# Scaling one head of two in an attention kernel, and turning a unit's first tile one slot earlier

## The reference

```python
x = x + tanh(g_xattn[0]) * attention(layernorm(x), ctx, ...)
x = x + tanh(g_ffn[0]) * ffn(layernorm(x), ...)
# attention, for every head h:
#   scores = q_r @ k_r^T              (64 wide)
#   attn   = softmax(scores)          (over 1024 keys)
#   ctx_c  = attn @ kv_rope           (128 wide)
# out = sum over h of (ctx_c @ w_kc_kv[h]^T) @ Wo[:, h]^T
```

## Time and profile before

| | |
|---|---|
| Median of 3 runs | 660.46 us (658.91 to 662.21) |
| The profiled execution | 660.33 us, span 658.5 us |
| TensorE busy | 637.6 us (97%) |
| VectorE busy | 538.6 us (82%) |
| GpSimd busy | 427.3 us (65%) |
| ScalarE busy | 420.3 us (64%) |
| Scaling on GpSimd (L1195) | 128 operations, 146.7 us |

### The profile page before, as it was taken

The page is one execution under the profiler, slowest core; times in us unless marked ns, Lnnn a source line. Parts: engine busy times, 40 slices in busy tenths (PEclk is TensorE's granted clock), DMA queues, the critical chain, the costliest instruction groups (busy, mean ns, idle before and its releaser), DMA issues.

```text
span 658.5 us, 10048 instructions
## 1 busy us (share of the span) xinstructions
PE 637.6 (97%) x2968; PEld 393.1 (60%) x2968; DVE 538.6 (82%) x870; ACT 420.3 (64%) x693; POOL 427.3 (65%) x368
## 2 busy tenths in 40 slices
PE   8799999999999999999999999999999999999997
PEld 7564556666766666666666646575655444445553
DVE  5777887788878887889798978898889986998863
ACT  2564686377747765766666756666665732598875
POOL 4834588767756775676578965776677254686651
PEclk9999999999999999999999999999999998999999
DMA  8208975888598949884988697878689671000001
GB/s 288 79 5 196 288 193 139 230 210 228 147 243 237 240 118 247 253 224 123 232 238 218 189 237 212 217 197 233 172 220 252 171 173 68 0 1 32 17 35 48
DMA packets 45208, 112.79 MB, mean 171 GB/s; under 512 B 11888, under 2 KB 15088, under 8 KB 45040
## 3 DMA queue, kind: packets, MB, share of 16 engines
q1 hardware_dynamic: 42128, 104.24, 59.8%
q10 hardware_dynamic: 2976, 8.06, 3.9%
q0 software_dynamic: 64, 0.00, 0.0%
HBM read 45.16 MB, written 2.10 MB: 72 GB/s over the span
## 4 chain that ended last, share of the span: by engine, by line
PE 56%; DVE 24%; issue 5%; ACT 5%; SPq 4%; DMA 3%; POOL 3%; PEld 1%; ACTq 0%; POOLq 0%; DVEq 0%; PEldq 0%
PE ps_s L1447 9%; DVE small L1853 7%; DVE E L1863 6%; PE ps_s L619 5%; PE ps_b L1480 5%; SPq L1129 4%; PE ps_ctx L1480 4%; PE ps_b L1343 3%; PE ps_b L1398 3%; PE ps_b L1345 3%; PE ps_b L1344 3%; ACT E L1676 2%; PE ps_b L1417 2%; PE ps_b L670 2%; DVE x_sb L1847 2%
## 5 line engine op out<-in xcount | busy, mean ns | idle before, releaser
L1195 POOL TENSOR_SCALAR E<-E,small 128x1024 f32<-128x1024 f32 x128 | 146.7, 1148 | 156.1 <-DVE small L1858 154.2
L1676 ACT ACTIVATE E<-ps_s,small 128x1024 f32<-128x1024 f32 x128 | 142.4, 1115 | 150.5 <-DVE small L1853 134.4
L1237 POOL TENSOR_TENSOR G_lo<-G,g_hi 128x512 fp32r<-128x512 f32 x130 | 168.2, 1308 | 6.7 <-ACT g_hi L1622 6.4
L1863 DVE STREAM_TRANSPOSE E<-E 128x1024 f32<-128x1024 f32 x124 | 152.4, 1231 | 21.8 <-POOL E L1195 21.5
L1853 DVE TENSOR_REDUCE small<-ps_s 128x1 f32<-128x1024 f32 x128 | 149.4, 1206 | 24.3 <-PE ps_s L1447 24.3
L1622 ACT ACTIVATE g_hi<-G 128x512 fp32r<-128x512 f32 x130 | 76.9, 632 | 3.9 <-DVE wq L1879 3.9
L1343 PE MATMUL ps_b<-b_hi,ctx_hi 128*128 128x512 f32 x128 | 66.5, 520 | 0.5 <-DVE ctx_lo L1819 0.3
L1480 PE MATMUL ps_b<-G,kv 128*128 128x512 f32 x126 | 64.7, 609 | 2.1 <-DMA G<-E 2.1
L1480 PE MATMUL ps_ctx<-G,kv 128*128 128x512 f32 x126 | 64.6, 607 | 0.3 <-POOL kv L1229 0.3
L1447 PE MATMUL ps_s<-k_hi,q_hi 64*128 64x512 f32 x256 | 57.3, 444 | 4.8 <-ACT E L1676 3.7
L619 PE MATMUL ps_s<-wq,q12T 128*128 128x512 fp8e4 x256 | 60.6, 383 | 0.1
(11 more groups left out here) (204 smaller groups left out, 1212.0 us busy)
## 6 DMA issues: line engine op xcount, KB each, us to landing
G<-E SPq DMA_DIRECT2D x496, 128.0 KB, 2.5
w_stage<-in_wffn SPq DMA_DIRECT2D x37, 512.0 KB, 4.7
w_stage<-in_wffn ACTq DMA_DIRECT2D x11, 512.0 KB, 4.6
wo_s<-in_woT SPq DMA_DIRECT2D x8, 512.0 KB, 5.2
wq_s<-in_wq SPq DMA_DIRECT2D x7, 512.0 KB, 4.9
wkcq_s<-in_wkcqT SPq DMA_DIRECT2D x7, 384.0 KB, 3.2
out<-x_sb SPq DMA_DIRECT2D x8, 256.0 KB, 2.0
x_sb<-in_x SPq DMA_DIRECT2D x3, 512.0 KB, 6.6
```

Of the source, the lines that this page charges most:

```text
L1195: nc.gpsimd.tensor_scalar(e, e, rowinv[:, k:k + 1], 1.0, ALU.mult, ALU.mult).then_inc(scaled, 1)
L1237: nc.gpsimd.tensor_tensor(g_tile(w % 2, i, G_lo), tile, high_part(i).bitcast(F32).rearrange("p (t i q) -> p t i q", t=ST, i=4), ALU.subtra ...
L1676: nc.scalar.activation(out, scores, ACT.Exp, bias=negmax[:, k:k + 1], accum_out=rowsum[:, k:k + 1]).then_inc(exp_done, 1)
L1863: nc.vector.transpose(e_tile(w % 2, t), e_tile(w % 2, t)).then_inc(blocks_turned, 1)
```

## The change

GpSimd scales the odd tiles alone, by the reciprocal of their own sum times the sum of the even tile beside them: the second head is brought to the scale of the first. The even tiles stay unscaled. Their reciprocals go to columns of their own, `row_scale`, one for each unit and half, and the output rows are multiplied by them when they are added to `x_sb` (`scaled_out`). The gate's tanh, which stood there, is multiplied into `b_hi` and `b_lo`. The transpose of an even tile waits for its exponential alone. `scaled` counts 8 for a pair where it counted 16.

In the order of the work two things move. VectorE turns u3's tile 0 at the end of the slot, behind its reciprocal and low(7), and no longer at the head of the next slot. The reciprocal of u2's tile 1 goes from the head of the slot to behind the maxima of tiles 2 and 3.

```diff
@@ -235,6 +238,7 @@
         negmax = small[:, 64:72]
         rowsum = small[:, 72:80]
         rowinv = small[:, 80:88]
+        row_scale = small[:, 25:33]
         ln_mv = small[:, 96:112].rearrange("p (t c) -> p t c", c=2)
         ln_rstd = small[:, 112:120]
         ln_eps = small[:, 120:128]
@@ -949,8 +953,7 @@
             for s in range(2):
                 dve.wait_ge(side_done, LAST_SIDE + s + 1)
                 x = x_sb[:, 6 + s, :]
-                nc.vector.scalar_tensor_tensor(x, ps_b[:, s, :], g_tanh[:, 0:1], x, ALU.mult, ALU.add)\
-                    .then_inc(side_freed if s == 0 else side_read, 1)
+                scaled_out(dve, PAIRS - 1, 3, s, ps_b[:, s, :], x).then_inc(side_freed if s == 0 else side_read, 1)
 
             dve.sem_inc(et_free, ET_FREE0)
@@ -1186,13 +1189,14 @@
             ffn_sp(sp)
 
 
-        def pool_scale(pool, p, w, t):
-
+        def pool_scale(pool, p, w, s):
+
+            t = 2 * s + 1
             e = first_e(t) if is0(p) and w == 0 else e_tile(w % 2, t)
             k = (w % 2) * ST + t
             pool.wait_ge(inv_done, 16 * p + (4 * w + t + 1))
             pool.sem_inc(pool_passed, 1)
-            nc.gpsimd.tensor_scalar(e, e, rowinv[:, k:k + 1], 1.0, ALU.mult, ALU.mult).then_inc(scaled, 1)
+            nc.gpsimd.tensor_scalar(e, e, rowinv[:, k:k + 1], rowsum[:, k - 1:k], ALU.mult, ALU.mult).then_inc(scaled, 1)
 
         def xn_half(i):
             b, h = divmod(i, 2)
@@ -1239,14 +1243,13 @@
 
         def pool_pair(pool, p, last=False):
             for w in range(4):
-                second, first = not (last and w >= 2), not (last and w >= 1)
-                u2, u3 = unit_ahead(p, w, 2), unit_ahead(p, w, 3)
+                second, u2 = not (last and w >= 2), unit_ahead(p, w, 2)
                 if splits(p, w):
                     split_low(pool, p, w, 0)
                 if splits(p, w):
                     split_low(pool, p, w, 1)
                 if second:
-                    pool_scale(pool, *u2, 1)
+                    pool_scale(pool, *u2, 0)
                 if last and w == 0:
                     join_kv(pool, 1)
                 if splits(p, w):
@@ -1256,8 +1259,7 @@
                 if last and w == 3:
                     rms_root(pool, 1)
                 if second:
-                    pool_scale(pool, *u2, 2)
-                    pool_scale(pool, *u2, 3)
+                    pool_scale(pool, *u2, 1)
                 if last and w == 2:
                     rms_root(pool, 0)
                     pool.wait_ge(ld_g, 32)
@@ -1275,8 +1277,6 @@
                     split_kv(pool, KV_SPLIT_SLOTS.index(w))
                 if isinstance(p, int) and (p, w) == (PAIRS - 2, 3):
                     join_kv(pool, 0)
-                if first:
-                    pool_scale(pool, *u3, 0)
                 if last and w == 1:
                     atanh_end(pool)
@@ -1320,13 +1320,9 @@
             root(2)
             normed_row(6)
             normed_row(7)
-            for t in range(ST):
-                pool_scale(pool, 0, 0, t)
-            pool_scale(pool, 0, 1, 0)
-            pool_scale(pool, 0, 1, 1)
-            pool_scale(pool, 0, 1, 2)
-            pool_scale(pool, 0, 1, 3)
-            pool_scale(pool, 0, 2, 0)
+            for w in range(2):
+                for i in range(2):
+                    pool_scale(pool, 0, w, i)
             pool_pair(pool, 0)
             with pool.Fori(1, XN_JOIN_PAIR) as p:
                 pool_pair(pool, p)
@@ -1589,7 +1585,8 @@
             task(6)
             pe.wait_ge(xnt_copied, 6)
             task(7)
-            pe.wait_ge(scaled, ST)
+            pe.wait_ge(exp_done, ST)
+            pe.wait_ge(scaled, 2)
             pe.wait_ge(xnt_copied, 8)
             first_turn(0)
             first_turn(1)
@@ -1638,7 +1635,9 @@
             elif kind == "a":
                 last = copy_act(a_hi[:, :, :].rearrange("p c r -> p (c r)"), bank_in)
             else:
-                last = copy_act(b_hi[:, task[1], :], bank_in)
+                if is0(p):
+                    act.wait_ge(gate_ready, 1)
+                last = nc.scalar.activation(b_hi[:, task[1], :], bank_in, ACT.Copy, scale=g_tanh[:, 0:1])
             last.then_inc(side_hi, 1)
 
         def xn_high_part(act, i):
@@ -1818,6 +1817,11 @@
 
             return nc.vector.tensor_tensor(out, full, hi.bitcast(F32), ALU.subtract)
 
+        def scaled_out(dve, p, u, i, bank_in, x):
+
+            dve.wait_ge(inv_done, 16 * p + (4 * u + 2 * i + 1))
+            return nc.vector.scalar_tensor_tensor(x, bank_in, row_scale[:, 2 * u + i:2 * u + i + 1], x, ALU.mult, ALU.add)
+
         def side_low(dve, p, variant, task, bank_in, at=None, hi_at=None):
 
             kind = task[0]
@@ -1841,10 +1845,11 @@
                 rows = query_rows(task)
                 last = lo_part(q_lo[:, task[1], rows], bank_in[:, 0:rows.stop - rows.start], q_hi[:, task[1], rows])
             elif kind == "b":
-                last = lo_part(b_lo[:, task[1], :], bank_in, b_hi[:, task[1], :])
+                last = nc.vector.scalar_tensor_tensor(b_lo[:, task[1], :], bank_in, g_tanh[:, 0:1], b_hi[:, task[1], :].bitcast(F32),
+                                                      ALU.mult, ALU.subtract)
             else:
                 x = x_sb[:, 2 * task[1] + task[2], :]
-                last = nc.vector.scalar_tensor_tensor(x, bank_in, g_tanh[:, 0:1], x, ALU.mult, ALU.add)
+                last = scaled_out(dve, p - 1 if task[1] == 3 else p, task[1], task[2], bank_in, x)
             last.then_inc(side_freed, 1)
 
         def max_tile(dve, p, w, t):
@@ -1855,11 +1860,15 @@
         def inv_tile(dve, p, w, t):
             dve.wait_ge(exp_done, 16 * p + (4 * w + t + 1))
             k = (w % 2) * ST + t
-            nc.vector.reciprocal(rowinv[:, k:k + 1], rowsum[:, k:k + 1]).then_inc(inv_done, 1)
+            inv = rowinv[:, k:k + 1] if t % 2 else row_scale[:, 2 * w + t // 2:2 * w + t // 2 + 1]
+            nc.vector.reciprocal(inv, rowsum[:, k:k + 1]).then_inc(inv_done, 1)
 
         def turn_blocks(dve, p, w, t):
 
-            dve.wait_ge(scaled, 16 * p + (4 * w + t + 1))
+            if t % 2:
+                dve.wait_ge(scaled, 8 * p + (2 * w + t // 2 + 1))
+            else:
+                dve.wait_ge(exp_done, 16 * p + (4 * w + t + 1))
             nc.vector.transpose(e_tile(w % 2, t), e_tile(w % 2, t)).then_inc(blocks_turned, 1)
 
         def ctx_low(dve, p, w):
@@ -1898,10 +1907,6 @@
                                 round_half(dve, q, g)
 
                 queries = (task_before(variant, w, 1) or ("",))[0] == "q"
-                if second:
-                    inv_tile(dve, *u2, 1)
-                    if not opening:
-                        turn_blocks(dve, *u2, 0)
                 low(0)
                 if variant == "last":
                     ffn_dve_early(dve, w, 0)
@@ -1914,6 +1919,8 @@
                 if second:
                     max_tile(dve, *u2, 2)
                     max_tile(dve, *u2, 3)
+                if second:
+                    inv_tile(dve, *u2, 1)
                 if opening:
                     turn_blocks(dve, *u2, 0)
                     turn_blocks(dve, *u2, 1)
@@ -1957,6 +1964,8 @@
                 if first:
                     inv_tile(dve, *u3, 0)
                 low(7)
+                if first:
+                    turn_blocks(dve, *u3, 0)
                 if variant == "last":
                     ffn_dve_early(dve, w, 7)
```

## The result

The changed kernel took 666.72 us, the median of 5 runs (666.15 to 670.59), against 660.36 for the kernel before: a ratio of 1.0101, with an interval of 1.0075 to 1.0128. That is 6.4 us slower where 0.8 was forecast, and 2.2 above the end of the range. The profiled execution is one of the two long ones, 669.21 us with a span of 667.4; the three runs at a granted clock of 1.000 took 666.15, 666.23 and 666.72.

A forecast was written before the change was run, and what follows sets the result against it. The prediction took the attention part to be bound by TensorE until the last pair of heads, with VectorE close behind. Its terms, -0.9 + 0.5 + 1.2 = +0.8 us, gave 661.2 us, range 657.5 to 664.5.

The forecast's parts named there:

- The forecast wait: VectorE ahead of tile 1's transpose: 1.2 us dead in slots 0 and 2, waits for GpSimd staying near 20 us.
- rival C: GpSimd's scaling with two columns is slow, 1.55 us, so the dead wait is 1.6: 662.8 us, chance 0.12.
- Start of pair 1: Low parts behind GpSimd's scaling start 1.1 us earlier and both TensorE gaps close: -0.9 us, bounds 0 and -1.0.
- The mean's product: Slot 3 of a summing pair: the x_sb row the mean waits for comes later, +0.5 us once, bounds 0 and +0.75.
- The last pair: Slot 1's new dead wait delays the transposes and the last exchange: +1.2 us, bounds +0.8 and +1.7.
- Three us of cover: GpSimd's low part of key tile 2, done by 432.3, wanted by TensorE at 435.28: the 1.4 us delay stays hidden.
- In slots bound by TensorE this costs nothing: VectorE's moved wait costs nothing where TensorE is packed, as long as exponentials are ready for the next scores.
- the 0.5 us of room given to the scores: Next slot 0 in a quantising pair: a 0.3 us shift of the exponentials is hidden, over 0.5 isn't.
- rival D: VectorE's dead wait passes the scores' room; TensorE waits for exponentials in the middle pairs: 664.7 us, chance 0.12.
- slot 0 wins 1.2 back at its head: The head wait of slot 0 goes in every pair, gaining 1.2 us: the argument against rival D.
- The list of gaps: TensorE gaps that a shift on VectorE or GpSimd could close: 0.5, 0.33, 0.69, 1.67 and 2.15, in all 5.3 us.
- Rival B: VectorE sets the pace from 392 us on and its 21.5 us of waits are mostly saved: 655.1 at best, chance 0.09.

The follow-up runs named there:

- scale3_short: The changed kernel with GpSimd's scaling of tile 3 cut to 32 of its 1024 columns: 663.49 us, 661.1 at full clock.
- fill_behind: inv1_head with an idle 1.2 us maximum on VectorE behind the reciprocal of tile 3, ahead of the transpose of tile 2: 668.73 us.
- turn2_short: The changed kernel with VectorE's transpose of tile 2 cut to 32 of its 1024 columns: 663.70 us, 662.1 at full clock.
- turn0_short: The changed kernel with the transpose of the first tile, at the end of the slot, cut to 32 of 1024 columns: 668.07 us, 666.5 at full clock.
- both_short: The changed kernel with the cuts of scale3_short and turn2_short together: 654.84 us; its control, the same cuts in inv1_head, took 652.66 us.
- inv1_head: The changed kernel with the reciprocal of tile 1 put back at the head of VectorE's slot: 654.7 us, ratio 0.9909 to the kernel before.
- arith_only: The changed kernel's arithmetic in VectorE's old order, reciprocal of tile 1 and transpose of tile 0 both back at the head: 654.85 us.
- lows_first: The changed kernel with GpSimd's low parts of key tiles 2 and 3 ahead of the scalings of tiles 1 and 3: 664.91 us.
- after_again: The changed kernel, unaltered, run and profiled once more: 670.08 us, 666.13 in the one run at full clock.

## Why the prediction was wrong

**The forecast wait was right.** 64 scalings of 1.205 us, median (1.2 was taken, bounds 1.1 and 1.55); VectorE stands 1.2 us ahead of tile 1 in slots 0 and 2, 25 us in sum ("near 20"). The prediction's estimate of 1.54 us, worked out from the Trainium skill ("GPSIMD Engine Reference", section "Performance versus the Vector engine"), is not met by the 1.205 measured, and rival C falls.

**The single terms mostly were, some by halves.** Start of pair 1: true gaps 0.50 and 0.33 before, 0.26 and none after, so -0.6 of the -0.9 there. The mean's product:

```profile
305.79 0.40 PE L1472 MATMUL ps_b<-G_lo,kv_hi 128*128 128x512 f32 x1
307.22 0.37 PE L1491 MATMUL ps_b<-small 128*128 128x24 f32 x2 [1.02 <-DVE x_sb L1823]
```

The true gap is 1.19, against 0.69: +0.5, as forecast. The last pair:

```profile
512.25 1.10 PE L1476 MATMUL ps_ctx<-G,kv 128*128 128x512 f32 x2 [0.63 <-POOL kv L1233]
...
529.43 0.50 PE L1443 MATMUL ps_s<-k_hi,q_hi 64*128 64x512 f32 x2 [0.92 <-ACT E L1675]
...
553.04 1.59 PE L1476 MATMUL ps_b<-G,kv 128*128 128x512 f32 x2 [1.91 <-DMA G<-E]
```

The scores that waited 1.67 us at 512.62 start at 520.10 without a wait. Over the whole pair the shift against before grows from 8.3 us (the scores at 505.87 against 497.56) to 8.9 (553.04 against 544.11): +0.6 for a forecast +1.2. The sign that was named for it, a wait of over 3 us ahead of the last exchange's products, didn't come: that wait is 1.91 us (truly 2.07), near the 2.15 before. Two waits that the prediction didn't list are here: kv, whose halves GpSimd joins behind the late scaling (0.63; 0.28 before, at 503.17), and the scores of slot 1.

**The step that failed is "Three us of cover".** It read GpSimd's room once, in slot 3, at the low part of key tile 2, and took it for every slot. The row of work behind that low part, a scaling and two more low parts, was not followed to TensorE. In slot 2 it ended 0.05 us ahead of its use before the change. The prediction itself gave the price for that case: without cover the delay "would fall on TensorE in every slot". So a term was put at nothing that is several us. The gaps ahead of low-part products alone are 3.2 us, and taking 1.1 us out of that row (scale3_short) gives back 5.1 at full clock.

**"In slots bound by TensorE this costs nothing" failed as well**, with the 0.5 us of room given to the scores. fill_behind and turn2_short show that VectorE has a share: the stretch from the maxima to the transpose of tile 3 has no room for 1.2 us. By which path it reaches TensorE in the changed kernel is open. Behind that stretch stand the exchange and the next maxima, hence the exponentials. In fill_behind TensorE waits for exponentials, which is rival D's mechanism (0.12). In the changed kernel D's sign is missing: between 120 and 529 us no scores have idle time of 0.15 us or more ahead of them, and the waits left for VectorE's lateness are those for b_lo, x_sb and the exchanges. The dead wait at the head that went was no counterweight: turn0_short shows that time just ahead of the head is free, so "slot 0 wins 1.2 back at its head" was worth little or nothing.

Together: the late reciprocal costs 11.5 us (666.2 against 654.7 at full clock). One cut gives back 5.1, the other 4.1, both 11.5, of which 2.0 are what they give where nothing is late. That the late reciprocal costs this much, and that time on both engines must be given back to undo it, is shown. An exact split is not: the two delays feed each other, and the stall before 458 goes with either cut. both_short also stays 2.1 us above its control (654.7 against 652.7 at full clock), where at most 1 was expected; that stays open.

**The arithmetic was priced at -0.9 and gains 5.5.** The list of gaps took the stretches to 304 and from 392 and left out the one between, where the kernel before has 2.2 us of idle time. 1.54 of it (truly 1.86) is a stall that inv1_head reduces to 0.57 (truly 0.73). Before:

```profile
388.66 1.12 PE L1480 MATMUL ps_b<-G,kv 128*128 128x512 f32 x2 [0.15 <-DMA G<-E]
391.18 3.27 PE L1417 MATMUL ps_b<-xn_rows,a_full 128*128 128x512 f32 x7 [1.39 <-DVE b_lo L1819]
```

inv1_head:

```profile
388.46 2.84 PE L1413 MATMUL ps_b<-xn_rows,a_full 128*128 128x512 f32 x6 [0.57 <-DVE b_lo L1848]
```

That stall is 1.1 us of the gain. By the last exchange inv1_head is 3.5 us ahead of the kernel before (540.62 against 544.11), and the other 1.7 of the 5.2 between the two profiles is the lower clock that follows in the kernel before. Runs of it at full clock are also 5.5 behind; where those lose is not shown. Rival B, VectorE's waits saved and gaps closing, had 655.1 at best and 0.09 for a chance. The 654.85 of arith_only, where the wait doesn't move, is close to that, but its list of gaps was another one, so the nearness of the numbers is partly luck.

## What to carry to other kernels

Before a wait is moved, follow the whole row of work queued behind it on its engine to the last consumer, in each kind of slot: the room at the first item says nothing of the fourth. An engine at 54% can have no room in the one stretch between a late input and a fixed due time, and VectorE's time, free at the head of the slot, cost up to 0.5 us for each 1.2 put in between the maxima and the last transpose (14 us over 29 slots in fill_behind, the lower clock's part included). To test which of two coupled delays costs, take time out at each place alone and at both, with a control that takes it out where nothing is late; reordering mostly renamed the wait. And look at each cut's profile for where its gain arises: here over half of it was one stall for an exchange.

## What the hardware showed beyond that

A pause of TensorE can cost more than itself. In the kernel before, the last exchange's wait (544.11, true gap 2.15) is followed by a lower granted clock. The rows are the profile cut into stretches of 5 us; the clock is the third number from the end.

```profile
540.00:545.00 5.00, 2.91 (x13) 1.23 (x12) 4.89 (x13) 1.51 (x2) 0.70 (x1) 0.91 0.93 244
545.00:550.00 5.00, 5.00 (x21) 2.16 (x20) 4.13 (x17) 0.69 (x2) 1.11 (x2) 0.74 0.29 115
```

In inv1_head a gap of 1.89 in the same place leaves it at full speed.

```profile
540.00:545.00 5.00, 4.38 (x21) 2.25 (x22) 4.72 (x21) 0.87 (x2) 1.14 (x2) 1.00 0.57 213
```

That isn't a matter of length alone: in lows_first the same wait is truly 2.19 us (at 550.56), and the clock stays.

```profile
550.00:555.00 5.00, 4.44 (x21) 2.25 (x22) 4.72 (x21) 0.94 (x2) 1.13 (x2) 1.00 0.62 213
```

In after_again two gaps of 1.39 and 1.70 us, 2.7 us apart, put the engine at the lower of its two levels (0.50, 1.2 GHz) for the whole of one such stretch:

```profile
392.14 1.12 PE L1476 MATMUL ps_b<-G,kv 128*128 128x512 f32 x2 [1.23 <-DMA G<-E]
394.81 5.49 PE L1413 MATMUL ps_b<-xn_rows,a_full 128*128 128x512 f32 x6 [1.54 <-DVE b_lo L1848]
```

```profile
390.00:395.00 5.00, 2.23 (x6) 0.57 (x5) 1.93 (x5) 2.81 (x6) 0.00 (x0) 0.89 0.95 193
395.00:400.00 5.00, 5.00 (x6) 2.00 (x7) 2.25 (x3) 3.72 (x7) 2.53 (x2) 0.50 1.03 211
400.00:405.00 5.00, 5.00 (x20) 2.47 (x19) 1.95 (x2) 1.49 (x3) 0.00 (x0) 0.93 1.04 245
```

Summed over the stretches that is 3.4 us of full-speed time lost there and 1.75 in the kernel before. Yet the profiled run of the changed kernel paused for 1.25 and 1.70 us at 461 and 464 and kept its full clock, and lost 1.7 us only behind its last exchange (0.86 and 0.80 in the two stretches from 550). So these rows don't give a rule. The spread goes with it: the changed kernel took 666.2 at a mean clock of 1.000, 669.2 at 0.997 and 670.6 at 0.995. The clock's own part of the last two is an estimated 2 and 3 us (0.3% and 0.5% of the time), so most of the spread. The last finding is the price that the prediction lacked. The scaling with two columns as factors took 1.205 us for 1024 elements, 7% above the 1.127 with one column and a constant.
